# The last five reciprocal square roots of a gated delta-rule layer, shared between VectorE and ScalarE

## What is computed

```python
def _layernorm(x, axis=-1, eps=1e-05):
    m = jnp.mean(x, axis=axis, keepdims=True)
    v = jnp.var(x, axis=axis, keepdims=True)
    return (x - m) / jnp.sqrt(v + eps)
...
        _, o = jax.lax.scan(step, S0, (tm(q), tm(k), tm(v), tm(g), tm(beta)))
        o = jnp.moveaxis(o, 0, 1)
        var = jnp.mean(jnp.square(o.astype(jnp.float32)), axis=-1, keepdims=True)
        o = o * jax.lax.rsqrt(var + NORM_EPS).astype(o.dtype) * norm_w
        gate = (x @ Wg.T).reshape(B, T, H, DV)
        o = o * jax.nn.silu(gate)
        return o.reshape(B, T, H * DV) @ Wo.T
...
        x_q = ternary_quantize(x, TH_X, SC_X)
        w_q = ternary_quantize(weight, TH_W, SC_W)
        w_rram = w_q + rram_variation
        return jnp.einsum('bsd,od->bso', x_q, w_rram)
    x = L0_attn_hidden_states
    x = _layernorm(x + _L0_attn_ref(x, ...), axis=-1)
    x = _layernorm(x + _L0_ffn_ref(x, L0_ffn_weight, L0_ffn_rram_variation), axis=-1)
    return x
```

## Time and profile before

| | |
|---|---|
| median of three runs | 350.73 us (350.22 to 351.06) |
| the profiled execution, its own time | 353.02 us |
| its span, first to last instruction | 351.2 us |
| mean granted TensorE clock | 0.86 |
| TensorE busy (matmuls) | 252.8 us, 72% |
| VectorE busy | 268.5 us, 76%, 660 instructions |
| ScalarE busy | 146.8 us, 42%, 271 instructions |

### The profile page before, as it was taken

The page is one execution under the profiler, slowest core; times in us unless marked ns, Lnnn a source line. Parts: engine busy times, 40 slices in busy tenths (PEclk is TensorE's granted clock), DMA queues, the critical chain, the costliest instruction groups (busy, mean ns, idle before and its releaser), DMA issues.

```text
span 351.2 us, 15117 instructions
## 1 busy us (share of the span) xinstructions
PE 252.8 (72%) x6956; PEld 178.0 (51%) x6956; DVE 268.5 (76%) x660; ACT 146.8 (42%) x271; POOL 9.2 (3%) x14
## 2 busy tenths in 40 slices
PE   2978943986479958958699589776928458967571
PEld 1435421666455535756455356665607357755441
DVE  0688999563999995969999887589999960546966
ACT  1497763255463602734636214635423024024031
POOL 2110000001000000010000000100000000000000
PEclk9999976698989985999989955999876757969898
DMA  7900000000000002000001020000010002000101
GB/s 231 359 0 2 3 1 0 4 4 6 4 5 4 0 0 63 6 4 6 6 4 60 0 63 4 4 7 4 4 60 0 2 5 63 6 5 4 60 1 60
DMA packets 8031, 9.82 MB, mean 28 GB/s; under 512 B 1568, under 2 KB 7072, under 8 KB 7968
## 3 DMA queue, kind: packets, MB, share of 16 engines
q1 hardware_dynamic: 6480, 8.39, 7.2%
q10 hardware_dynamic: 1488, 0.47, 0.5%
HBM read 6.76 MB, written 2.10 MB: 25 GB/s over the span
## 4 chain that ended last, share of the span: by engine, by line
PE 53%; DVE 22%; issue 18%; ACT 5%; DMA 1%; DVEq 0%; SPq 0%; ACTq 0%
PE fr L322 15%; PE pj L335 10%; PE pj L350 5%; PE pg L322 5%; PE pc L322 4%; DVE conv_buf L958 4%; PE po L322 3%; PE pc L479 3%; PE po L479 2%; PE pj L509 2%; DMA xt<-x_t 1%; PE pj L367 1%; DVE tok_buf L970 1%; DVE ss L991 1%; DVE stats L1222 1%
## 5 line engine op out<-in xcount | busy, mean ns | idle before, releaser
L335 PE MATMUL pj<-xt,wproj 128*128 128x512 f32 x96 | 53.6, 706 | 8.4 <-DMA xt<-x_t 6.4
L958 DVE SCALAR_TENSOR_TENSOR conv_buf<-raw,wconv,conv_buf 128x512 f32<-128x512 f32 x72 | 53.3, 755 | 4.9 <-ACT conv_buf L663 3.2
L335 PEld LDWEIGHTS pj<-xt,wproj 128*128 128x128 f32 x96 | 20.0, 220 | 31.0 <-issue 24.0
L662 ACT ACTIVATE raw<-pj 128x512 f32<-128x512 f32 x24 | 14.3, 596 | 34.7 <-PE pj L335 34.7
L1088 DVE TENSOR_TENSOR mq<-fr,ad 128x512 f32<-128x512 f32 x12 | 8.3, 692 | 26.5 <-PE fr L322 26.5
L350 PE MATMUL pj<-xt,wproj 128*128 128x512 f32 x48 | 25.1, 664 | 4.6 <-ACT conv_buf L663 4.6
L322 PE MATMUL fr<-x_t,x 32*32 32x16 f32 x768 | 11.5, 209 | 21.6 <-issue 21.6
L322 PEld LDWEIGHTS fr<-x_t,x 32*32 32x32 f32 x768 | 10.9, 151 | 24.3 <-issue 24.3
L322 PE MATMUL fr<-kga,wu 32*32 32x64 f32 x768 | 14.7, 228 | 7.2 <-issue 7.2
L350 PEld LDWEIGHTS pj<-xt,wproj 128*128 128x128 f32 x48 | 10.0, 213 | 16.4 <-issue 8.4
L727 ACT ACTIVATE s_sb<-po 128x192 f32<-128x192 f32 x12 | 4.0, 330 | 32.8 <-PE po L322 32.8
(11 more groups left out here) (181 smaller groups left out, 578.2 us busy)
## 6 DMA issues: line engine op xcount, KB each, us to landing
xt<-x_t SPq DMA_DIRECT2D x1, 1536.0 KB, 11.4
res<-x SPq DMA_DIRECT2D x3, 512.0 KB, 4.1
out<-hid_buf SPq DMA_DIRECT2D x6, 256.0 KB, 2.1
wproj<-w_proj SPq DMA_DIRECT2D x1, 1024.0 KB, 7.4
xt<-x_t SPq DMA_DIRECT2D x1, 512.0 KB, 5.0
kq<-x SPq DMA_DIRECT2D x1, 512.0 KB, 3.8
wout<-w_out SPq DMA_DIRECT2D x1, 384.0 KB, 11.7
cst<-consts ACTq DMA_DIRECT2D x1, 305.5 KB, 11.4
```

The lines of the kernel that those rows point to most:

```text
L335: mm = pe.matmul(pj[:, j % 2, :], wproj[:, t, j * P:(j + 1) * P], xt[:, t, k * TOK:(k + 1) * TOK], start=(t == 0), stop=(t == KT - 1))
L662: act.activation(raw[:, j, :, TAPS - 1:], bank, ACT.Copy)
L958: e = dve.scalar_tensor_tensor(out=conv[:, d, :, :], in0=raw[:, d, :, m:m + T], scalar=wconv[:, j, m:m + 1], in1=conv[:, d, :, :], op0=ALU ...
```

## The change

In the ending, five of the six reciprocal roots are made in another way: the one of the head outputs of half s = 1 (number 0), those of the first norms of s = 0 and s = 1 (numbers 1 and 2), and those of the second norms of s = 0 and s = 1 (numbers 3 and 4). VectorE takes a reciprocal (`end_inverse` tells ScalarE), ScalarE takes its square root (`end_root` tells VectorE), and VectorE makes one Newton step. The head outputs of s = 0 keep the nine instructions, as do all roots of the turns.

```diff
         UF = U // 2
+        root_args = ([(r_all[:, 0:UF], t_all[:, 0:UF])] + [(r_n[:, p], t_n[:, p]) for p in
+                                                           (slice(0, 2), slice(2, 4), slice(0, 2), slice(2, 4))])
...
+        end_inverse, end_root = (sem(n) for n in ("end_inverse", "end_root"))
...
-            for s in range(2):
-                end_first(s)
-                end_move(s)
+            def end_square_root(i):
+                act.wait_ge(end_inverse, i + 1)
+                act.activation(root_args[i][0], root_args[i][1], ACT.Sqrt).then_inc(end_root, 1)
+
+            end_square_root(0)
+            end_square_root(1)
+            end_first(0)
+            end_move(0)
+            end_square_root(2)
+            end_first(1)
+            end_move(1)
+            end_square_root(3)
             end_second()
+            end_square_root(4)
...
+            def end_rsqrt(i, v):
+
+                y, t = root_args[i]
+                dve.reciprocal(t, v).then_inc(end_inverse, 1)
+                dve.wait_ge(end_root, i + 1)
+                rsqrt_newton(y, v, t, 1.0)
...
-            def end_factors(bank, s):
+            def end_factors(bank, s, i):
...
-                rsqrt(r_n[:, pair], v_n[:, pair], t_n[:, pair])
+                end_rsqrt(i, v_n[:, pair])
...
-                end_factors(y_bank[s], s)
+                end_factors(y_bank[s], s, 1 + s)
...
-                end_factors(fr[:, s, :], s)
+                end_factors(fr[:, s, :], s, 3 + s)
...
-                rsqrt(head_r[s], head_v[s], t_all[:, 0:UF])
+                if s:
+                    end_rsqrt(0, head_v[s])
+                else:
+                    rsqrt(head_r[s], head_v[s], t_all[:, 0:UF])
```

## The result

| | before | after |
|---|---|---|
| median of 20 runs each, taken together | 349.86 us (347.26 to 351.33) | 348.29 us (344.32 to 351.25) |
| span of the profiled execution | 351.2 us | 345.4 us |
| VectorE instructions | 660 | 635 |
| ScalarE instructions | 271 | 277 |
| the ending, by its profile | 24.32 us | 23.63 us |

The ratio of after to before is 0.994, with a 95% interval of 0.9912 to 0.9967. The changed kernel is faster by 1.6 us by the medians; the prediction had 0.6 us less than before, 350.1 us, with a range of 349.1 to 351.2.

A forecast was written before the change was run, and what follows sets the result against it. Only the ending counts, its chain almost wholly on VectorE, with TensorE running close beside it. First norms + 0.53, second norms - 0.38 and - 0.76 sum to - 0.61 us: 350.1 us from 350.73, range 349.1 to 351.2.

The forecast's parts named there:

- So I carry the difference over: 350.73 - 0.6: Final step: the ending's saving of 0.6 us is taken off the earlier median of 350.73, giving 350.1 us.
- Root 0, + 1.06 us: Head outputs of s = 1: table load waits behind ScalarE's four normalizations, so the scaling begins 1.06 us later.
- The small root at 1.02 us: Each norm root, when nobody is late: 1.02 us against 1.78, at most 0.76 saved.
- 2.76 behind po's end: First norms of s = 1: the shift begins 2.76 us after the second output projection (po) ends on TensorE.
- Of the savings of roots 1 and 2 nothing else is left: First norms: root 1 hidden behind projection po, root 2 behind the copy; the shift comes 0.53 us later.
- po at 5.0 us: Second output projection on TensorE, partly at low clock after a pause: 5.0 us, between 4.49 and 5.50.
- Roots 1 and 3: Norms of s = 0: first hidden behind projection po; second saves 0.38 us of 0.76, the second feed-forward covering the rest.
- Root 4: Second norm of s = 1: saves the whole 0.76 us, since only its own output and the last DMAs follow.
- the full clock for po: Rival: second output projection takes 2.75 us at full clock; sum - 1.60, 349.1 us; chance 0.08.
- the lasting low clock: Rival: TensorE still at 1.2 GHz for residual and transposes behind projection po; + 1.31, 352.0 us; chance 0.06.
- The longer load: Rival: table load holds ScalarE a second stretch of about 1.28 us before root 0; + 0.67, 351.4 us; chance 0.08.
- the dearer handoff: Rival: each handoff between VectorE and ScalarE costs 0.1 us more a way; - 0.2, 350.5 us; chance 0.06.

The follow-up runs named there:

- root 0 alone: Against the kernel before, only the head root of s = 1 is made the new way, the norms' four keep nine instructions; 348.66 us, ratio 1.005.

## Why the prediction was wrong

**The direction and the mechanism held; the time and the size did not.** The forecast was - 0.61 us and 350.1; measured were - 1.57 us between the medians and 348.29.

- **"So I carry the difference over: 350.73 - 0.6": this step failed most.** The starting point was the median of three runs within 0.8 us, and I took "the spread of a median of few runs (0.4 us here)" for the scatter of the kernel. Twenty runs of the same program have 349.86, 35 on one chip have 347.45 and 35 on another 349.34, and single runs lie 7.65 us apart on the first of these (343.87 to 351.52). The prediction also took 0.2% as the least change that a measurement tells; the intervals were 0.3% to either side with 20 runs of each kernel and up to 0.5% with 12 against 35. The sum gave 350.12 and 348.29 was measured: 0.87 of the 1.83 us of the miss is the first of these shifts (350.73 to 349.86), and the other 0.96 is the larger change (- 1.57 in place of - 0.61). The trace could have warned me: it showed a granted clock that changes all along a chain that is 53% TensorE.
- **Root 0, + 1.06 us: right.** + 1.06 in the profile, with the load at 1.28, 0.02 behind the last normalization (318.40 + 2.06 to 320.48) and 0.01 ahead of the root. The page of the Trainium skill "ScalarE: Activation LUTs" (What ACT_TABLE_LOAD costs) has a drain of about 1380 ns besides; no run here shows one.
- **The small root at 1.02 us: right,** 328.25 to 329.27, with reciprocals of 0.17 and 0.23 and a square root of 0.20. The handoff back was 0.04 (328.65 to 328.69).
- **"2.76 behind po's end": the term that was mis-sized.** It measured 2.43 us in three profiles. 0.18 of the surplus is the 0.88 us from po's end to the transposes, which in the earlier trace rows was set by VectorE's ternary values and not by TensorE; freed of them it was 0.70 (332.35 to 333.05). 0.13 is the wait behind the copy: I let square root 2 start 0.02 after the copy's end, but an instruction that waits for nothing in the copy started 0.11 before it (333.97 against 334.08). So the copy costs root 2 0.09 us and not 0.5, and the sentence "Of the savings of roots 1 and 2 nothing else is left" was wrong for root 2: it gave 0.68 of its 0.76 (1.10 in place of 1.78).
- **po at 5.0 us: inside the range taken,** 4.54, 5.24 and 5.41. But the sum set it against a kernel before with po at 4.49, whose cover held. With po at 5.49 before is itself 0.3 us longer. The reason given, an idle time of 5.2 us, held in two profiles of three; in the one with 4.54 it was 3.52.
- **Roots 1 and 3: right in the main.** Root 1 is hidden by po where po is long, and root 3 is worth 0.38: shown by taking each back, in one execution each. By the sum's own numbers root 1 was not quite hidden (without it VectorE is ready at 337.50, and po ends at 337.27), which does not alter the sum. Root 4 takes 1.02 in place of 1.78, and nothing stands behind it to hide the saving; it was not taken back by itself.
- **The sum, corrected:** po's end 1.06 later and 0.75 longer in the first pair of profiles, 2.43 to the shift, - 0.38 and - 0.76, is - 0.70; the profile had - 0.69. That this is close to the forecast of - 0.61 is partly luck: po took 0.24 us more than the 5.0 in the sum, and the way behind it 0.33 less. The two profiles before average 24.47 us and the three after 23.45, so the ending is worth about 1.0 us; single pairs give 0.5 to 1.7.
- **What stays open:** whether the 1.57 us between the medians hold more than the ending. The three sets have ratios of 0.994, 0.9966 and 0.9953, each with an interval that reaches 0.9967 or beyond, so that none excludes a change of 1.2 us. Nothing in the profiles shows an effect ahead of the edits, and the variation there is larger than what is left over. The changed kernel is faster (two of the three intervals lie wholly below 1, and all three profiled endings are shorter); by how much the runs don't say to within 0.5 us.

Of the rivals, the full clock for po and the lasting low clock did not come in these profiles of the changed kernel (the latter did, for one step, in root 0 alone, and for a part of the residual where root 1 was taken back). The longer load is refuted (0.01 us from its end to the root), and the dearer handoff too (0.03 us there and 0.04 back).

## What to carry to other kernels

A short serial step moved to another engine costs what stands in that engine's order ahead of it: here a table load of 1.28 us behind 2.06 us of unrelated work turned one root from a gain of 0.73 us into a loss of 1.06, and putting the step ahead of that work took it back. Ask of each saving what TensorE or a copy has still to finish at that point; the saving of root 1 went there where po was long, and half of root 3's. And take the scatter of a kernel from many runs, or compare the one stretch that was edited, when the rest of its chain hangs on a clock that moves.

## What the runs showed of the hardware

A pause of 5.2 us on TensorE was followed by 4.35 us of work at 1.2 GHz; with 4.31 us of added matmuls in the pause, which left 1.06 us of it, the same twelve instructions took 2.86 us in place of 5.24. The grant did not always fall: behind a pause of 2.10 us they took 2.86 as well. The pause alone did not fix their time: behind 4.15 and 4.16 us they took 4.49, 5.49 and 4.34 us. On ScalarE an instruction that waited for nothing started about 0.1 us before the end of the one ahead (the root behind the copy at 333.97 against 334.08; two normalizations of 0.56 us take 1.02 together), so that a queue of short ones was a little cheaper than the sum of their durations. The table load did not overlap so: it began 0.02 us after the end of the instruction ahead.
